# Layer 2 of a four-layer graph network: sums taken one quad later and values scaled in place, with an early mask load, later weight loads and an output stored by rows

## The reference, cut to what matters

```
layer 1:  agg = einsum('ij,jf->if', adj == 1, x) / deg;  agg @ W.T + b
layer 2:  h = x @ W;  e = leaky(h @ a_src + (h @ a_dst).T)
          elu(softmax(where(adj > 0, e, -1e12)) @ h)
layer 3:  S = (x @ Wq) @ (x @ Wk).T;  softmax(S masked by adj + eye) @ (x @ Wv)
```

## Time and profile before

| | |
|---|---|
| median of 3 runs | 2343.1 us (2340.27 to 2345.26) |
| the profiled execution's own time | 2346.69 us |
| its span | 2345.0 us |
| mean granted TensorE clock | 0.984 |
| layer 0 with its opening | 0 to 921.5 us |
| layer 1 | to about 1207.5 us |
| layer 2 | to about 1632.8 us |
| layer 3 | to 2345.0 us |

### The profile page before, as it was taken

One profiled execution on the slowest core, in us unless ns is written; L12 is line 12 of the kernel. 1 busy time (PEld: TensorE's weight loads), 2 busy tenths in 40 slices (PEclk: granted clock), 3 DMA queues, 4 the chain that ended last, 5 costly groups with the idle time before them and its releaser, 6 DMA issues. The chain is left out here.

```text
span 2345.0 us, 45615 instructions
## 1 busy us (share of the span) xinstructions
PE 2225.0 (95%) x17180; PEld 1701.0 (73%) x17180; DVE 1798.9 (77%) x2845; ACT 1372.6 (59%) x2100; POOL 114.6 (5%) x124
## 2 busy tenths in 40 slices
PE   5799999999999998999978999999999999999998
PEld 4677767778677776888867888887466666666667
DVE  6877788797877855212249999997898898898896
ACT  6555565665656565666655555554365565665556
POOL 2000010010100001000000000000000000000000
PEclk9899999999999999999989999999999999999999
DMA  7542340414321112222211222222111011111000
GB/s 178 113 64 37 64 82 32 82 46 82 56 62 47 39 57 84 83 89 89 89 38 58 68 67 72 79 73 85 54 37 50 26 52 52 35 46 50 25 30 28
DMA packets 62934, 146.72 MB, mean 63 GB/s; under 512 B 10023, under 2 KB 14778, under 8 KB 61757
## 3 DMA queue, kind: packets, MB, share of 16 engines
q1 hardware_dynamic: 56461, 110.57, 15.2%
q0 software_dynamic: 5760, 33.56, 8.7%
q10 hardware_dynamic: 560, 0.52, 0.1%
HBM read 170.30 MB, written 41.43 MB: 90 GB/s over the span
## 5 line engine op out<-in xcount | busy, mean ns | idle before, releaser
L193 PE MATMUL bank<-s_row,kT_hi 128*128 128x512 f16 x1024 | 308.0, 383 | 5.3 <-ACT arena L2038 3.1
L2152 PE MATMUL bank<-VB,arena 128*128 128x257 f16 x1024 | 281.8, 275 | 26.1 <-DVE arena L2078 20.1
L1560 PE MATMUL bank<-VA,ph 128*128 128x257 f16 x1024 | 281.2, 275 | 8.7 <-DVE VA L1169 8.7
L2859 PE MATMUL bank<-VA,w_dense 128*128 128x257 f16 x1024 | 280.7, 274 | 3.0 <-ACT w_dense L2683 2.4
L1562 PE MATMUL bank<-VA,pl 128*128 128x257 f16 x1024 | 280.8, 274 | 0.0
L1561 PE MATMUL bank<-VA,ph 128*128 128x257 f16 x1024 | 280.8, 274 | 0.0
L2155 PE MATMUL bank<-VB,arena 128*128 128x257 f16 x1024 | 280.7, 274 | 0.0
L2153 PE MATMUL bank<-VB,arena 128*128 128x257 f16 x1024 | 280.6, 274 | 0.0
L2861 PE MATMUL bank<-VA,arena 128*128 128x257 f16 x1024 | 280.2, 274 | 0.0
L2860 PE MATMUL bank<-VA,w_dense 128*128 128x257 f16 x1024 | 280.2, 274 | 0.0
L2017 ACT CAST arena<-arena 128x512 f16<-128x512 f32 x256 | 155.8, 617 | 153.4 <-DVE arena L2069 144.1
(11 more groups left out here) (344 smaller groups left out, 4935.9 us busy)
## 6 DMA issues: line engine op xcount, KB each, us to landing
mask<-mask_d SPq DMA_DIRECT2D x128, 256.0 KB, 2.7
arena<-mask_d SPq DMA_DIRECT2D x128, 256.0 KB, 2.7
mask_d<-in_adj POOLq DMA_DIRECT2D x8, 2048.0 KB, 23.4
xg<-in_x SPq DMA_DIRECT2D x8, 512.0 KB, 12.8
x<-xg SPq DMA_DIRECT2D x8, 512.0 KB, 3.9
xg<-x SPq DMA_DIRECT2D x8, 512.0 KB, 4.3
x<-xo POOLq DMA_DIRECT2D x8, 512.0 KB, 3.0
w_dense<-x SPq DMA_DIRECT2D x8, 512.0 KB, 4.3
```

The costliest lines, as they stand in the source:

```text
L193: last = nc.tensor.matmul(out_ap, st, mv, start=(i == 0), stop=(i == len(todo) - 1))
L1560: nc.tensor.matmul(acc, ph[:, u % HR, c], v_row(V, 0, t), start=(t == 0), stop=False)
L2152: nc.tensor.matmul(acc, p_hi, v_at(V, 0, t), start=first, stop=False)
L2859: nc.tensor.matmul(acc, ph[:, u % ring, j, c], v_row(V, 0, t), start=(t == 0), stop=False)
```

## The change

Five things are joined.

1. **Layer 2's group boundary.** `late` is 1: ACT's four `ag`, `below` and `e` all follow quad 1's casts. DVE does all four weight tiles of quad 1, then `inverse` for blocks 0 to 2, the first `pl`, `inverse` for block 3, and the other `pl`.
2. **Early mask.** A buffer `quad_ring` of 8 KB a partition serves as layer 0's `p32` and as mask ring of layers 1 to 3. SP loads the mask of layer 1's quad 7 in layer 0, behind a wait for layer 0's last `pl`. PE takes this quad tile by tile and no longer waits for four casts.
3. **Later loads.** SP loads Wq and Wk after the loop of layer 1.
4. **Rows at the end.** PE does the last two pairs of layer 3 block by block; DVE inverts and scales and adds x in one pass of 256 columns out of PSUM for each block, and SP stores 128 KB for each.
5. **Values in place.** ACT multiplies the four rows of `wh` in place in float32 and casts 1024 columns into the value rows; DVE subtracts in one instruction of 1024 columns. PE's wait is for the quad's.

The diff, cut:

```diff
+        quad_ring = sb(top, "quad_ring", [P, R * GW], F32)
+        quad_masks = quad_ring[:, :].bitcast(U8).rearrange("p (a n) -> p a n", n=R * GW)
...
+        def four_values(V, part, q):
+            at = part * (T * VW) + q * (R * VW)
+            return V[:, at:at + R * VW].rearrange("p (r w) -> p r w", w=VW)[:, :, 0:D]
...
                             if i == G and q == 0:
                                 load_later()
+                                sp.wait_ge(low.sem, low.upto(G * T - 1))
+                                slot = NEXT % R
+                                sp.dma_start(quad_masks[:, slot, :], mask_d[0:P, NEXT * QW:(NEXT + 1) * QW]
+                                             ).then_inc(s_mask[slot], 16)
...
-                mask = quad_masks(arena[0]) if weighted else sb(mem, "mask", [P, MS, R * GW], U8)
+                mask = quad_masks
-                late = 0 if weighted else 0
+                late = 1 if weighted else 0
...
                     def quad(g, q):
                         eng, stage = (dve_q, "p32") if weighted else (act_q, "hi")
+                        if not weighted and isinstance(g, int):
+                            return
...
-                    groups(sp, quad, work["sync"], None, work.get("sync_between"))
+                    groups(sp, quad, work["sync"], None, None, work.get("sync_beside"))
...
                         for t in range(q * R, q * R + R):
-                            nc.scalar.mul(v_row(V, 0, t, D), wh[:, t * D:(t + 1) * D], vprime[:, t:t + 1]
-                                          ).then_inc(v_hi.sem, 1)
+                            nc.scalar.mul(wh[:, t * D:(t + 1) * D], wh[:, t * D:(t + 1) * D], vprime[:, t:t + 1]
+                                          ).then_inc(v_scaled.sem, 1)
+                        act.wait_ge(v_scaled.sem, v_scaled.upto(q * R + R - 1))
+                        nc.scalar.copy(four_values(V, 0, q), four_rows(wh[:, q * R * D:(q + 1) * R * D])
+                                       ).then_inc(v_hi.sem, 1)
 
                     def part(act, g, q):
-                        if q == 0:
+                        if q == late:
                             work["sums_free"](act, g)
...
                         for r in range(R):
                             dve.wait_ge(dve_q.sem, dve_q.before(n, "lo", r))
-                            if r == 2 and q == 1 and not isinstance(g, int):
-                                inverse(g - 1, R - 1, R)
...
                         for r in range(R):
+                            if r == 1 and q == late and not isinstance(g, int):
+                                inverse(g - 1, R - 1, R)
                             dve.wait_ge(act_q.sem, act_q.at(n, "hi", r))
...
-                            for t in range(q * R, q * R + R):
-                                dve.wait_ge(v_hi.sem, v_hi.upto(t))
-                                nc.vector.scalar_tensor_tensor(
-                                    out=v_row(V, 1, t, D), in0=wh[:, t * D:(t + 1) * D], scalar=vprime[:, t:t + 1],
-                                    in1=v_row(V, 0, t, D), op0=ALU.mult, op1=ALU.subtract).then_inc(v_lo.sem, 1)
+                            dve.wait_ge(v_hi.sem, v_hi.upto(q))
+                            nc.vector.tensor_tensor(
+                                four_values(V, 1, q), four_rows(wh[:, q * R * D:(q + 1) * R * D]), four_values(V, 0, q),
+                                ALU.subtract).then_inc(v_lo.sem, 1)
...
                     def middle(g, q):
+                        if q == late and not isinstance(g, int) and weighted:
+                            inverse(g, 0, R - 1)
...
-                                pe.wait_ge(v_lo.sem, v_lo.upto(q * R + r))
+                                pe.wait_ge(v_lo.sem, v_lo.upto(q))
...
                     def quad(g, q):
-                        if q == Q - 1 or (q == 0 and not weighted):
+                        own = isinstance(g, int) and not weighted
+                        if (q == Q - 1 and not own) or (q == 0 and not weighted):
                             return quad_by_rows(g, q)
...
+                for r in range(R):
+                    sp.wait_ge(end_rows.sem, end_rows.upto(r))
+                    sp.dma_start(out[(G - 1) * P:G * P, r * D:(r + 1) * D], row(res, r)).then_inc(s_end, 16)
...
+                def end_row(r):
+                    dve.wait_ge(end_summed.sem, end_summed.upto(r))
...
+                    nc.vector.reciprocal(rden[:, r:r + 1], bank[4 + r][:, D:D + 1]).then_inc(end_inverted.sem, 1)
+                    dve.wait_ge(end_inverted.sem, end_inverted.upto(r))
+                    nc.vector.scalar_tensor_tensor(out=row(res, r), in0=bank[4 + r][:, 0:D], scalar=rden[:, r:r + 1],
+                                                   in1=row(xg, r), op0=ALU.mult, op1=ALU.add).then_inc(end_rows.sem, 1)
...
+                def end_values(pair_list):
+                    pe.wait_ge(low.sem, low.upto(pair_list[-1]))
+                    for i in range(R):
...
-                    for n in range(head, total + depth):
+                    for n in range(head, total + depth - 2):
                         step(n)
+                    end_values([total - 2, total - 1])
```

More of the change, by code:

```diff
@@ L1881, in build @@
         Q = T // R
-        MASKS = MS * R * GW // 4
-        ARENA = MASKS + 11 * R * GW // 2
+        ARENA = 11 * R * GW // 2
         arena = []
-        def quad_masks(t):
-            return t[:, 0:MASKS].bitcast(U8).rearrange("p (a n) -> p a n", a=MS)
         def cuts(t, at):
@@ L1935, in aggregate @@
                         "omega_exp", "gam_exp", "v_exp", "omega_scaled", "gam_scaled", "v_column"))
[L1936 to L1937 removed]
+                    gam_spread, gam_rowed, v_scaled, v_hi, v_lo = (Count(sem(f"l2_{n}")) for n in (
+                        "gam_spread", "gam_rowed", "v_scaled", "v_hi", "v_lo"))
                 work = side(mem, ag)
@@ L2105, in part @@
                             middle(g, q)
-                        if q == 0:
-                            inverse(g, 0, R if isinstance(g, int) or not weighted else R - 1)
+                        if q == 0 and (isinstance(g, int) or not weighted):
+                            inverse(g, 0, R)
                         work["dve"](dve, g, q)
@@ L2179, in quad @@
                                 last = tile_row(q, r, i)
+                                if q * R + r == T - 1 and i < R - 1:
+                                    last.then_inc(pe_r.sem, pe_r.one("row", i))
                             last.then_inc(pe_q.sem, pe_q.one("pv", r))
@@ L2250, in finish_layer1, with sync_beside @@
             qk_turned, qkT_hi, qkT_lo, qk_made = (Count(sem(n)) for n in ("qk_turned", "qkT_hi", "qkT_lo", "qk_made"))
-            def sync_between():
+            def sync_beside(q):
+                if q >= 0:
+                    return
                 for i, src in enumerate(("L3_gnn_Wq", "L3_gnn_Wk")):
@@ L2543, in fused_attention @@
             pl = cut([ring, 2, GW], F16)
-            mask = arena[0][:, 0:slots * QW // 4].bitcast(U8)
+            mask = quad_ring[:, 0:slots * QW // 4].bitcast(U8)
             rden = sb(top, "rden", [P, R], F32)
@@ L2699, in step @@
                         row_of_tops(g - 1)
-                    if p == 2 and g >= 2:
+                    if p == 2 and 2 <= g <= G:
                         rows_out(g - 2)
@@ L2803, in rest @@
                         step(n)
-                    rows(G - 1)
+                    for r in range(R):
+                        end_row(r)
                 def step(n):
@@ L2863, in values @@
                     last.then_inc(summed.sem, 1)
+                def end_values(pair_list):
+                    pe.wait_ge(low.sem, low.upto(pair_list[-1]))
+                    for i in range(R):
+                        acc = bank[4 + i][:, 0:D + 1]
+                        c = slice(i * P, (i + 1) * P)
+                        for u in pair_list:
+                            for j in range(2):
+                                t = 2 * (u % pairs) + j
+                                nc.tensor.matmul(acc, ph[:, u % ring, j, c], v_row(V, 0, t), start=False, stop=False)
+                                nc.tensor.matmul(acc, ph[:, u % ring, j, c], v_row(V, 1, t), start=False, stop=False)
+                                last = nc.tensor.matmul(acc, pl[:, u % ring, j, c], v_row(V, 0, t), start=False,
+                                                        stop=(t == T - 1))
+                        last.then_inc(end_summed.sem, 1)
                 def turn(g):
```

25 lines of the change are left out of this document (16 added, 9 removed).

## The result

The changed kernel takes **2319.7 us** (median of four runs, 2318.1 to 2321.1) against 2343.9 for the kernel before in the same series (2340.3 to 2345.3): a ratio of 0.9899, 95% interval 0.9882 to 0.9916. A second series of both gave 2320.5 and 2342.2. The gain is 24.2 us in the first series and 21.7 in the second; I had forecast 17.1, and a range of 2319 to 2334 us that 2319.7 only just reaches. Over all 56 executions of the kernel before that were timed the median is 2342.7, over all nine of the changed kernel 2319.9: 22.8 us.

A forecast was written before the change was run, and what follows sets the result against it. PE was busy for 95% of the span, so only its idle time, clock losses and the tail could be won. Terms of 4.0, 2.0, 7.2, 0.5 and 3.4 made 17.1 us, taking median 2343.1 to 2326.0 us; range 2319 to 2334.

The forecast's parts named there:

- DVE has slack in the loop: Layer 2's six later boundaries: DVE was to have 1.1 us of slack in a group of 49.8 us.
- Layer 1 begins: Start of layer 1: with the mask ready early, PE starts at 922.6 and 4.0 us are won.
- its bound of 4.9: Start of layer 1: upper bound of the 4.0 us term, with full clock from 925.2 on.
- My sentence that the clock may rise sooner: Start of layer 1: the term was rounded up to 4.0 us since the clock may rise sooner than assumed.
- Group 0 and the first boundary: Layer 2: shorter DVE quads and waits removed, less a 3.9 us wait for `ag`: 2.0 us won, bounds 0 and 3.5.
- the first rival: Layer 2: ACT binds, group 0 wins nothing, a boundary wins 0.8 us; 12.7 us in all, 2330.4; chance 0.13.
- Six boundaries: Layer 2's other boundaries: PE's wait falls from 2.42 to 1.2 or 1.3 us, 7.2 us won, bounds 3 and 13.
- Layer 3 begins: Start of layer 3: DVE half a microsecond further ahead of PE, 0.5 us won, bounds 0 and 1.
- The end: Behind the last matmul: only block 3 left, SP stores 128 KB; 3.4 us won, range 2.5 to 4.2.
- my bound of 4.2: Behind the last matmul: upper bound in us of the 3.4 us term.
- The third rival: Layers 1 and 2: PE keeps its clock, half-clock stretches go, 3.2 us more won, 2322.8; chance 0.08.
- The slower rival: Layer 2: DVE never regains its lead, every boundary waits 3.9 us for `ag`; 13.8 us slower, 2356.9; chance 0.03.

The follow-up runs named there:

- a third cut: PE makes q and v behind quad 4 instead of quad 5, against the changed kernel with x later and group 0's values' low part first: 2312.7 us.

## Why the prediction was right, and which terms were off

The sign held, and the five parts did in kind what was forecast. The range held by less than 1 us, at its edge: the gain was larger than 17.1 us because three terms were too small. One reading behind a term, that DVE has slack in the loop, was wrong. By terms:

- **Layer 1 begins, 4.0 forecast.** From the last matmul of layer 0 to one fixed matmul ahead of layer 2 (1189.38 before, 1182.57 after) it is 271.7 against 267.1 us: 4.6, and 4.6 again in the second pair of executions. PE's wait is 5.0 as forecast. The step that was off is the clock: I let half speed last until 928.6, and at 924 the window shows full speed; PE then waits 0.6 us for `ag`, which keeps the gain below its bound of 4.9. My sentence that the clock may rise sooner was right.
- **Group 0 and the first boundary, 2.0.** DVE's quads are 6.19 us (6.2 forecast), the first `ag` wait is 3.6 (3.9). I had written that PE begins 1.9 us later, but waits between quads anyway; the wait grew from 3.12 to 5.80 us, or by 1.8 against the kernel with the values as before. Taken with the 4.3 us that follow, the scaling is worth 2.5 at group 1's first matmul, as forecast. That 1.0 is left of it at group 2's, against the run with the values as before, is the place where the clock fell. I had it fall at 1274, behind the first boundary's wait; it did, at 1269. The in-place products did not bind ACT, the first rival's mechanism.
- **Six boundaries, 7.2.** They gave 6 x 1.48 = 8.9. The wait for `ag` was put at 1.2 to 1.3 and is 0.84 to 0.92, so a group takes 49.58 us where I had 49.8. DVE's idle time I read as 1.1 us of slack. It is 1.03 us, but the runs show something else in slack's place: 0.70 of it was for the exponential and 0.30 for DVE's own results, and these waits and PE's 0.91 lie on one ring of waits. A cut at either (`ag` earlier, `x` later) gave 0.1 us a group at most; a third cut, on top of the second, gave 0.5.
- **Layer 3 begins, 0.5.** 3.08 to 2.70 and 3.15 to 2.57: 0.4 to 0.6. DVE begins the step on the mask piece (`own_entries`) 0.96 us ahead of the end of PE's last sum, before 0.57: the lead grew by 0.4, as forecast.
- **The end, 3.4.** 4.9, above my bound of 4.2 (and 2345.0 less 2341.5 is 3.5, not 3.4). The arithmetic came out (0.7 us behind the last matmul, 0.72 measured). The store was mis-sized: 2.4 us to landing where 1.8 is measured, and 1.2 us for closing taken over from POOL's store where 0.4 is left: from DVE's last row (2315.78) to the end of the span (2318.0) it is 2.2 us in all. Before, the same distance is 4.75 (2340.25 to 2345.0). The Trainium skill (DMA: Bandwidth & Descriptors, anatomy of one DMA) gives 2.3 us for 128 KB, an estimate. Its fit is for transfers that GpSimd issues, and this store is SP's, so the measured 1.8 says nothing against it.

By these, 4.6, 2.5, 8.9, 0.5 and 4.9, less 0.5 for the first boundary (3.6 us of waiting against 0.66 for `ag` and 2.42 for a low part before), make 20.9 us. The spans differ by 20.6 in the first pair and by 21.1 in the second, once the two rows of the table that the change leaves alone are taken out. The medians of all executions differ by 22.8. The rest, 1.9 us, would fit the clock in untouched places, of which the first profiled execution of before carried 6.4 us, but no run shows it for the medians. The medians of the four parts undone one at a time add up to 26.0 us, more than the whole: the part of the values alone stands in it with 4.7 us where its rows show 2.5 at most.

The third rival (PE keeps its clock) put 3.2 us more on the gain. Its number, 2322.8, is nearer to the result than my 2326.0, but the trace bears it out only where layer 1 begins, where full clock was back at 924. In layer 2 the clock falls behind one boundary before and behind one after the change in the first pair of executions, and behind two, 1284 and 1336, in the second execution of before. The slower rival, a boundary that is each time like the first, did not come: 0.91 us, not 3.6.

The Trainium skill (TensorE: Matmul & The Clock Gate, what is actually happening) has the clock fall with idleness. In layer 2 the trace agrees as far as the half clock seen at 1289 and at 1336 stands behind a boundary's wait of 2.4 us. But the same wait stands at seven places in each execution of before, and the clock fell behind one of them in the first and behind two in the second. So these runs show that such a wait can be followed by half clock, and not that it always is.

## What to carry to other kernels

An engine's idle time in a loop is slack only if it ends on the engine that sets the pace. Follow each wait round the loop until you are back: here ACT's `ag` hung on DVE, DVE on ACT's exponential and cast, these on PE's products 9 us earlier, and a cut at `ag` or at `x` gave next to nothing before a further one (products one quad earlier, on top of `x` later) gave 3 to 4 us. Before explaining a gain by a profile, take a second profile of the unchanged kernel and look at a stretch that the change can't reach.

## What the runs showed of the hardware that I had not expected

The places where PE drops to half clock differ between executions of one program with the same waits at the boundaries, and moved by 6.4 us what one execution showed for two stretches that no edit touched. Such a loss can also cost nothing: 1.7 us of it hid in a wait for `ag` that was then 2.16 us and not 3.9. A store of 128 KB from SP landed after 1.8 us and the span ended 2.2 us behind DVE's last row, where 512 KB through POOL took 4.75 us from the same point: 0.59 us to the issue (2340.25 to 2340.84), 0.53 for it, and the transfer with the closing.
